# Moving the value bias's product and the key weights' split from the start of the attention stage into the last feed-forward tile

## The chip, the cores and the metric

The kernel runs on one core of one Trainium2 chip. The metric is the time on the device in microseconds (us), as the median of several runs. TensorE is the matrix engine, VectorE, ScalarE and GpSimd are the three engines for elementwise work, and SyncE's queue issues the DMA transfers. In the profile they are PE (with PEld for its weight loads), DVE, ACT, POOL and SP.

## The reference

The input x has 8192 tokens of 512 features. It is normalised, and an attention part and a feed-forward part are added to it:

```
xn  = (x - mean) / sqrt(var + 1e-5)
qkv = xn @ Wqkv + bqkv          # 16 heads of 32
att = softmax(mask(q @ k.T) / sqrt(512)) @ v      # blocks of 128 tokens, each sees itself and its neighbours
h   = bitlinear(xn, w_fc) + gate * (xn @ v.T @ fast_b.T @ u.T)
out = x + (att @ Wout + bout) + bitlinear(relu(h)**2, w_proj)
```

The bias of the values passes through the softmax unchanged, because each row of the softmax sums to one. So the kernel adds it once, as `v_bias @ Wout + bout`, to every token.

## The kernel before

The work runs in three parts, one after the other. A preparation rounds and transposes the feed-forward weights. The feed-forward stage then goes over 16 tiles of 512 tokens and writes x plus its result to the array `partial` in HBM. The attention stage goes over 128 steps (32 pairs of blocks times 4 groups of 4 heads) and adds its own result. A stage is a block in which each engine has an instruction list of its own. No engine starts the next stage before all engines have ended the last one, and SyncE's list in the feed-forward stage ends with waits for all of its stores (L597 to L599).

Every float32 product is made of rounded parts. An operand is split into a high part, rounded by a ScalarE copy, and a low part, which VectorE or GpSimd gets by subtraction. Three products of such parts are then added (hi times hi, lo times hi, hi times lo).

**The feed-forward tile.** It has 16 steps. In step s TensorE makes nine matmuls for `up` (L749 to L753) and, two steps behind, eight for `down` (L763, L765). ScalarE makes `relu` (L643) and the high part of the square (L636). VectorE makes the square (L704) and its low part (L687). At the end of a tile `take_down` (L695, VectorE) scales the four 128-row blocks of `down_ps` into `y`. GpSimd adds the residual x to each block (L611), and SyncE stores each block (L583, for the last tile L596). The first tile and the last tile stand outside the loop, so they can hold instructions of their own. The attention weights `wqkv_raw`, `wout_raw` and the biases are loaded during the first tile.

**The start of the attention stage.** SyncE loads the transposed tokens (L986): first the high part and the low part of block 0, then four more pairs. VectorE spreads the value bias into `v_bias_wide` (L1287). TensorE multiplies it with `wout_raw` in strips of 32 columns (L1523), and VectorE adds `bout_wide` (L1295). Meanwhile ScalarE rounds the keys', the values' and the queries' third of `wqkv_raw`, 128x2048 elements each (L1169), and then `wout_raw` (L1171). VectorE makes the three low parts (L1292), and GpSimd that of `wout` (L1078). After its bias product TensorE makes the keys of block 0 (L1533, 48 matmuls), the values of block 0 (L1362, 12), two jobs of queries and keys (L1353, 48 in all) and the values of block 1 (L1362, 12). Then come the first scores (L1440).

```
            pe.wait_ge(w_lo_done, 1)
            pe.wait_ge(x_here[(-1) % XR], 32)
```

These two waits stand ahead of L1533. The first is for the keys' split and the second for the tokens of block 0.

Of the kernel before, what the change touches and what calls it, by code (L numbers as in the profile page):

```python
# [14 lines left out]
F32 = mybir.dt.float32  # L15
# [7 lines left out]
P = 128  # L23
D = 512
# [426 lines left out]
def feed_forward_stage(nc, x, fast_b, w_fc, w_proj, u, v, gate, xT_dram, x_turned_dram, partial, weights):  # L451
# [13 lines left out]
    with ExitStack() as ctx:  # L465
# [44 lines left out]
        down_ps = ctx.enter_context(nc.psum_tensor("down_ps", [P, NB, D], F32))  # L510
        low_ps = ctx.enter_context(nc.psum_tensor("low_act_ps", [3 * DH, T], F32))

# [7 lines left out]
        xT_stored = [sem(f"xT_stored{b}") for b in range(NB)]  # L520
        block = ctx.enter_context(nc.Block())

        NORM_STEP = [2, 2, 3, 3]
# [21 lines left out]
        def _(sp):  # L545
# [55 lines left out]
        @block.gpsimd  # L601
        def _(pool):
            def tile(i, par):

                if not is_last(i):
                    for b in range(NB):
                        inverse_std(pool, nc, stats[:, b, :], minus_half, ln_step[b], 5 * (i + 1) + 3)
                for b in range(NB):
                    pool.wait_ge(down_taken, NB * i + b + 1)
                    pool.wait_ge(part_here[b], 16 * (i + 1))  # L610
                    nc.gpsimd.tensor_tensor(y[:, b, :], y[:, b, :], part_in[:, b, :], ALU.add).then_inc(y_done, 1)  # L611

            tiles(pool, tile)

        @block.scalar
        def _(act):
# [11 lines left out]
            def low_high(i, par):  # L628
                act.wait_ge(low_filled, i + 1)
                nc.scalar.copy(low[:, par, :], low_ps[:, :]).then_inc(low_hi_done, 1)  # L630

# [6 lines left out]
            def tile(i, par):  # L638
                for s in range(FB):
# [21 lines left out]
        def _(dve):  # L661
# [36 lines left out]
            def tile(i, par):  # L698
                for s in range(FB):
# [26 lines left out]
            square_lo(NT - 1, FB - 1)  # L726
            take_down(NT - 1)

        @block.tensor
        def _(pe):  # L730
            def low_rank(i, par):
# [3 lines left out]
                for n in range(2 * DC):  # L735
                    k, pass_ = divmod(n, 2)
                    a = xT_lo if pass_ else xT_hi
                    last = nc.tensor.matmul(low_ps[:, :], low_in[:, k, :], a[:, par, k, :],
                                            start=(n == 0), stop=(n == 2 * DC - 1))
# [40 lines left out]
            for s in range(FB - LAG, FB):  # L780
                down(NT - 1, s)


def attention_stage(nc, loaded, xT_dram, partial, turned_dram, pair_dram, out):
# [14 lines left out]
    with ctx:  # L799
# [7 lines left out]
        wqkv_here, wout_here, biases_here = loaded.arrived  # L807
        wqkv_hi = sb("wqkv_hi", [P, DC, 3 * D], F32R)
        wqkv_lo = sb("wqkv_lo", [P, DC, 3 * D], F32R)
        wout_hi = sb("wout_hi", [P, DC, D], F32R)  # L810
        wout_lo = sb("wout_lo", [P, DC, D], F32R)
        v_bias_wide = sb("v_bias_wide", [P, DC, P], F32)
        out_bias = sb("out_bias", [P, D], F32)
        mask = sb("mask", [P, 3 * P], F32)
# [29 lines left out]
        wout_hi_done, wout_lo_done = sem("wout_hi_done"), sem("wout_lo_done")  # L844
        wide_done, bias_summed, bias_added = sem("v_bias_wide_done"), sem("bias_summed"), sem("bias_added")
        zeroed, ident_done, mask_done = sem("ident_zeroed"), sem("ident_done"), sem("mask_done")
# [23 lines left out]

        SPLIT_ORDER = (1, 2, 0)

# [195 lines left out]
        def _(pool):  # L1068
# [6 lines left out]
                                    fill=NEG, base=0, pattern=[[-1, P]], channel_multiplier=1).then_inc(mask_done, 1)  # L1075
            pool.wait_ge(bias_summed, 1)
# [3 lines left out]
            pool.wait_ge(bias_added, 1)  # L1080

            def widen_inverse_sums(t, b):
# [38 lines left out]
        def _(act):  # L1121
# [44 lines left out]
            act.wait_ge(wqkv_here, 64)  # L1166
            for part in SPLIT_ORDER:
                cols = slice(part * D, (part + 1) * D)
                nc.scalar.copy(wqkv_hi[:, :, cols], wqkv_raw[:, :, cols]).then_inc(w_hi_done, 1)  # L1169
            act.wait_ge(wout_here, 16)  # L1170
# [29 lines left out]
        def _(dve):  # L1200
# [85 lines left out]
            dve.wait_ge(biases_here, 48)  # L1286
            nc.vector.tensor_copy(v_bias_wide[:, :, :], v_bias[:, :].unsqueeze(2).to_broadcast([P, DC, P])  # L1287
                                  ).then_inc(wide_done, 1)
            for n, part in enumerate(SPLIT_ORDER):
                cols = slice(part * D, (part + 1) * D)  # L1290
                dve.wait_ge(w_hi_done, n + 1)
                nc.vector.tensor_tensor(wqkv_lo[:, :, cols], wqkv_raw[:, :, cols],  # L1292
                                        wqkv_hi[:, :, cols].bitcast(F32), ALU.subtract).then_inc(w_lo_done, 1)
            dve.wait_ge(bias_summed, 1)
            nc.vector.tensor_tensor(out_bias[:, :], score_ps[:, 0, :], bout_wide[:, :], ALU.add).then_inc(bias_added, 1)  # L1295
            dve.wait_ge(mask_done, 2)
# [38 lines left out]
        def _(pe):  # L1335
# [7 lines left out]
            def project_qk(u, bank, first, last_):  # L1343

                i, c = where(u)
                for n in range(first, last_):
                    is_k, m = divmod(n, PASSES * DC)
                    k, x_low, w_low = pass_of(m)
                    w = wqkv_lo if w_low else wqkv_hi
                    a = xT_lo if x_low else xT_hi  # L1350
                    col = is_k * D + c * P
                    tokens = a[:, x_slot(i):x_slot(i) + 2, k, :] if is_k else own_tokens(a, i, k)
# [4 lines left out]
            def project_v(i, r, bank, first, last_):  # L1357
                for n in range(first, last_):
                    k, x_low, w_low = pass_of(n)
                    w = wqkv_lo if w_low else wqkv_hi  # L1360
                    a = xT_lo if x_low else xT_hi
                    last = nc.tensor.matmul(job_ps[:, bank, :], a[:, x_slot(i) + r, k, :], w[:, k, 2 * D:3 * D],  # L1362
                                            start=(n == 0), stop=(n == PASSES * DC - 1))
# [153 lines left out]

            pe.wait_ge(wide_done, 1)
            pe.wait_ge(wout_here, 16)
            for k in range(DC):  # L1520
                for g in range(HC):
                    strip = slice(g * DH, (g + 1) * DH)
                    last = nc.tensor.matmul(score_ps[strip, 0, :], v_bias_wide[:, k, strip], wout_raw[:, k, :],  # L1523
                                            start=(k == 0), stop=(k == DC - 1), tile_position=(0, g * DH))
            last.then_inc(bias_summed, 1)
            pe.wait_ge(w_lo_done, 1)
            pe.wait_ge(x_here[(-1) % XR], 32)
            for c in range(DC):
                for n in range(PASSES * DC):
                    k, x_low, w_low = pass_of(n)  # L1530
                    w = wqkv_lo if w_low else wqkv_hi
                    a = xT_lo if x_low else xT_hi
                    last = nc.tensor.matmul(job_ps[:, 0, c * P:(c + 1) * P], w[:, k, D + c * P:D + (c + 1) * P],  # L1533
                                            a[:, x_slot(-1) + 1, k, :], start=(n == 0), stop=(n == PASSES * DC - 1))
# [42 lines left out]
class AttentionWeights:  # L1577
# [3 lines left out]
    sources: tuple  # L1581
    tables: tuple
    arrived: tuple

# [22 lines left out]
def feed_forward(nc, x, partial, fast_b, w_fc, w_proj, u, v, gate, out):  # L1607
# [6 lines left out]
    with ExitStack() as ctx:  # L1614
# [3 lines left out]
        def sem(name):  # L1618
# [3 lines left out]
                                   (sb("wqkv_raw", [P, DC, 3 * D]), sb("wout_raw", [P, DC, D]),  # L1622
                                    sb("v_bias", [P, DC]), sb("qk_bias", [P, 2 * DC]), sb("bout_wide", [P, D])),
                                   (sem("wqkv_here"), sem("wout_here"), sem("biases_here")))
        feed_forward_stage(nc, x, fast_b, w_fc, w_proj, u, v, gate, xT_dram, x_turned_dram, partial, weights)
# [34 lines left out]
```

## Time and profile before

| | |
|---|---|
| median of 3 runs | 2405.69 us (2405.29 to 2405.75) |
| the profiled execution's own time | 2402.34 us |
| its span, first to last instruction | 2400.5 us |
| mean granted TensorE clock | 0.992 of full speed |
| TensorE busy | 2341.3 us (98%) |
| VectorE, ScalarE, GpSimd busy | 1675.9, 1374.2, 441.6 us |
| preparation and feed-forward stage | from 0 to 1095.2 us |
| attention stage | from 1095.2 us to the end |

Times in the rows are counted from the start of the span. The granted clock is a share of full speed: 1.00 is 2.4 GHz and 0.50 is 1.2 GHz. Instructions on one engine overlap a little at their ends, so the busy time of a group can be less than its count times its mean.

### The profile page before, as it was taken

How to read it: one execution, taken by the hardware profiler on the slowest of the kernel's cores; microseconds unless marked ns; L12 is line 12 of the kernel's file. 1: busy time of each engine (PE TensorE's matmuls, PEld its weight loads, DVE VectorE, ACT ScalarE, POOL GpSimd, SP SyncE). 2: the span in 40 equal slices, each digit the busy share in tenths (PEclk: the TensorE clock that was granted, in tenths of full speed). 3: DMA queues.
4: the chain of work that ended last, by engine and by line, in shares of the span. 5: the costliest groups of instructions: out<-in, count | busy, mean ns of one | idle time of the engine just before them, and what ended most of it. 6: DMA issues, size and time to landing. Idle time of an engine off the chain costs nothing.

```text
span 2400.5 us, 56237 instructions
## 1 busy us (share of the span) xinstructions
PE 2341.3 (98%) x19528; PEld 1912.8 (80%) x19528; DVE 1675.9 (70%) x4576; ACT 1374.2 (57%) x3488; POOL 441.6 (18%) x734
## 2 busy tenths in 40 slices
PE   6999999999999999998999999999999999999997
PEld 5888888888888888886788888888887888888885
DVE  6455544555545444535888888888888888988896
ACT  6333333333333333324777777777777777777775
POOL 2011111111111001102222222222222222222222
PEclk8999999999999999999999999999999999999999
DMA  5643344433344444314899999999999999999996
GB/s 188 206 113 110 102 114 122 117 102 109 110 122 122 114 113 122 105 36 133 261 293 296 292 296 291 290 300 283 298 289 294 293 292 288 294 291 290 291 286 191
DMA packets 390109, 495.74 MB, mean 207 GB/s; under 512 B 35792, under 2 KB 296400, under 8 KB 389888
## 3 DMA queue, kind: packets, MB, share of 16 engines
q1 hardware_dynamic: 389744, 492.71, 69.7%
q8 instruction: 129, 2.11, 0.4%
q14 instruction: 92, 0.75, 0.1%
q0 software_dynamic: 144, 0.17, 0.0%
HBM read 261.53 MB, written 231.21 MB: 205 GB/s over the span
## 4 chain that ended last, share of the span: by engine, by line
PE 27%; DMA 9%; ACT 7%; issue 4%; DVE 4%; SPq 2%; POOL 0%; POOLq 0%; DVEq 0%
PE job_ps L1353 8%; PE job_ps L1362 5%; PE job_ps L1513 5%; ACT wqkv_raw L1134 5%; PE score_ps L1440 4%; DMA turned_pairs<-pair_blocks 4%; DMA pair_moved<-turned_pairs 3%; PE job_ps L1371 3%; DVE wqkv_raw L1212 2%; PE pT_ps L1456 2%; SPq L1035 1%; DMA turned_blocks<-wqkv_raw 1%; ACT pT L1143 1%; DMA wqkv_raw<-turned_blocks 1%; ACT q_hi L1159 1%
## 5 line engine op out<-in xcount | busy, mean ns | idle before, releaser
L1134 ACT ACTIVATE wqkv_raw<-wqkv_raw,neg_max 128x384 f32<-128x384 f32 (+1 forms) x1024 | 619.3, 606 | 218.8 <-DVE neg_max L1212 215.8
L643 ACT ACTIVATE relu<-up_ps,fc_scale 128x512 f32<-128x512 f32 x256 | 176.1, 688 | 633.5 <-PE up_ps L753 633.5
L704 DVE SCALAR_TENSOR_TENSOR sq<-up_ps,relu 128x512 f32<-128x512 f32 x256 | 177.0, 692 | 494.5 <-ACT relu L643 493.3
L1212 DVE CUSTOM_DVE_ANT_0 wqkv_raw<-score_ps,mask 128x384 f32<-128x384 f32 (+1 forms) x1024 | 504.0, 549 | 25.1 <-PE score_ps L1440 24.2
L765 PE MATMUL down_ps<-proj_T,sq_lo 128*128 128x512 f32 x1024 | 404.7, 395 | 0.0
L763 PE MATMUL down_ps<-proj_T,sq_hi 128*128 128x512 f32 x1024 | 404.3, 395 | 0.2 <-DVE sq_lo L687 0.2
L749 PE MATMUL up_ps<-f_xT_hi,fc_T 128*128 128x512 f32 x1024 | 400.3, 391 | 2.2 <-PEq L136 2.2
L751 PE MATMUL up_ps<-f_xT_lo,fc_T 128*128 128x512 f32 x1024 | 400.3, 391 | 0.0
L1229 DVE STREAM_TRANSPOSE wqkv_raw<-wqkv_raw 128x384 f32<-128x384 f32 (+1 forms) x508 | 282.6, 573 | 66.9 <-ACT wqkv_raw L1134 64.2
L1353 PE MATMUL job_ps<-xT_hi,wqkv_hi 128*128 128x256 f32 x1024 | 309.9, 303 | 0.1
L1353 PE MATMUL job_ps<-xT_lo,wqkv_hi 128*128 128x256 f32 x1024 | 289.2, 282 | 0.0
L1353 PE MATMUL job_ps<-xT_hi,wqkv_lo 128*128 128x256 f32 x1024 | 288.9, 282 | 0.0
L611 POOL TENSOR_TENSOR f_y<-f_y,part_in 128x512 f32<-128x512 f32 x64 | 88.2, 1410 | 865.5 <-DVE f_y L695 865.5
L763 PEld LDWEIGHTS down_ps<-proj_T,sq_hi 128*128 128x128 f32 x1024 | 193.7, 189 | 45.6 <-DVE sq_lo L687 1.1
L765 PEld LDWEIGHTS down_ps<-proj_T,sq_lo 128*128 128x128 f32 x1024 | 192.8, 188 | 45.6
L749 PEld LDWEIGHTS up_ps<-f_xT_hi,fc_T 128*128 128x128 f32 x1024 | 192.7, 188 | 44.7 <-issue 2.4
L751 PEld LDWEIGHTS up_ps<-f_xT_lo,fc_T 128*128 128x128 f32 x1024 | 192.9, 188 | 43.5
L1087 POOL COPY rcp_wide<-sum_rcp 128x128 f32<-128x128 f32 x256 | 74.7, 292 | 805.7 <-DVE sum_rcp L1221 805.7
L1353 PEld LDWEIGHTS job_ps<-xT_lo,wqkv_hi 128*128 128x128 f32 x1024 | 196.3, 192 | 0.0
L1353 PEld LDWEIGHTS job_ps<-xT_hi,wqkv_hi 128*128 128x128 f32 x1024 | 195.5, 191 | 0.5 <-ACT values L1127 0.3
L1353 PEld LDWEIGHTS job_ps<-xT_hi,wqkv_lo 128*128 128x128 f32 x1024 | 195.3, 191 | 0.0
L1134 ACT ACTIVATION_READ_ACCUMULATOR wqkv_raw<-wqkv_raw,neg_max 128x1 f32 x1024 | 192.5, 188 | 0.0
(158 smaller groups left out, 4374.3 us busy)
## 6 DMA issues: line engine op xcount, KB each, us to landing
turned_blocks<-wqkv_raw SPq DMA_DIRECT2D x123, 768.0 KB, 4.8
wqkv_raw<-turned_blocks SPq DMA_DIRECT2D x492, 192.0 KB, 4.1
turned_pairs<-pair_blocks SPq DMA_DIRECT2D x124, 384.0 KB, 4.1
pair_moved<-turned_pairs SPq DMA_DIRECT2D x496, 96.0 KB, 3.3
xT_hi<-xT SPq DMA_DIRECT2D x65, 256.0 KB, 4.9
xT_lo<-xT SPq DMA_DIRECT2D x65, 256.0 KB, 5.0
xT<-f_xT_hi SPq DMA_DIRECT2D x64, 256.0 KB, 2.9
xT<-f_xT_lo SPq DMA_DIRECT2D x64, 256.0 KB, 3.1
```

The source lines that it names most:

```text
L643: nc.scalar.activation(relu[:, s % 2, :], up_ps[:, s % 2, :], ACT.Relu, scale=fc_scale2[:, s:s + 1]).then_inc(relu_done, 1)
L704: nc.vector.scalar_tensor_tensor(sq[:, s % 2, :], up_ps[:, s % 2, :], 0.0, relu[:, s % 2, :], ALU.max, ALU.mult).then_inc(sq_done, 1)
L749: nc.tensor.matmul(up_ps[:, s % 2, :], fc_T[:, k, cols], xT_hi[:, par, k, :], start=(k == 0), stop=False)
L751: nc.tensor.matmul(up_ps[:, s % 2, :], fc_T[:, k, cols], xT_lo[:, par, k, :], start=False, stop=False)
L763: nc.tensor.matmul(down_ps[:, b, :], sq_hi[:, s % 2, t], proj_T[:, s, :], start=(s == 0), stop=False)
L765: last = nc.tensor.matmul(down_ps[:, b, :], sq_lo[:, s % 2, t], proj_T[:, s, :], start=False, stop=(s == FB - 1))
L1134: nc.scalar.activation(probs[:, u, cols], probs[:, u, cols], ACT.Exp, bias=neg_max[:, u:u + 1], scale=-1.0, accum_out=prob_sum[:, u:u + 1] ...
L1212: nc.vector.tensor_tensor_reduce(out=probs[:, u, cols], in0=score_ps[:, h, cols], in1=mask[:, cols], scale=-SCORE_SCALE, scalar=3e38, op0= ...
L1229: nc.vector.transpose(blocks[:, :, seen.start:seen.stop, u, :].rearrange("p a w t -> p w a t"), probs[:, u, seen.start * P:seen.stop * P]. ...
L1353: last = nc.tensor.matmul(job_ps[:, bank, is_k * T:(is_k + 1) * T], w[:, k, col:col + P], tokens, start=(m == 0), stop=(m == PASSES * DC - 1))
L1362: last = nc.tensor.matmul(job_ps[:, bank, :], a[:, x_slot(i) + r, k, :], w[:, k, 2 * D:3 * D], start=(n == 0), stop=(n == PASSES * DC - 1))
L1513: last = nc.tensor.matmul(out_, values[:, blk % VR, head * DH:(head + 1) * DH], p, start=(w == seen.start), stop=(w == seen.stop - 1), til ...
```

## The change

- **Bias product.** `v_bias_wide` is made by VectorE in step 4 of the last feed-forward tile. TensorE makes the product after the last `down` step of that tile, as four matmuls over all 128 columns instead of sixteen over 32, into `low_ps`. VectorE adds `bout_wide` at the end of its list. In the attention stage L1287, L1523 and L1295 go.
- **Key weights.** ScalarE rounds the keys' third of the weights in four pieces of 128x512, in steps 4 to 7 of the last tile. VectorE makes the low part in four pieces in steps 5 to 8. The attention stage splits only values and queries.
- **Residual blocks.** Of the last tile's four blocks GpSimd adds 0 and 1. VectorE adds 2 and 3 after `take_down`. SyncE stores them in the order 0, 2, 1, 3.
- **Waits.** In the attention stage TensorE's waits for `wide_done` and `wout_here`, the first one for `w_lo_done`, and that for `bias_added` go, as do GpSimd's for `bias_summed` and `bias_added`.

```diff
@@ SyncE, feed-forward stage
-            for b in range(NB):
-                sp.wait_ge(y_done, NB * (NT - 1) + b + 1)
+            for b in (0, 2, 1, 3):
+                if b < 2:
+                    sp.wait_ge(y_done, NB * (NT - 1) + b + 1)
+                else:
+                    sp.wait_ge(late_y_done, b - 1)
                 sp.dma_start(block_rows(partial, NB * (NT - 1) + b), y[:, b, :]).then_inc(stored[b], 16)
@@ GpSimd
-                for b in range(NB):
+                for b in range(2 if is_last(i) else NB):
@@ ScalarE, step s
+                    if is_last(i) and 0 <= s - W_STEP < DC:
+                        act.wait_ge(wqkv_here, 64)
+                        nc.scalar.copy(wk_hi[:, s - W_STEP, :], wqkv_raw[:, s - W_STEP, KEY_COLS]).then_inc(w_rounded, 1)
@@ VectorE, step s
+                    if is_last(i) and s == W_STEP:
+                        dve.wait_ge(biases_here, 48)
+                        nc.vector.tensor_copy(v_bias_wide[:, :, :], v_bias[:, :].unsqueeze(2).to_broadcast([P, DC, P])
+                                              ).then_inc(wide_done, 1)
+                    if is_last(i) and 0 <= s - W_STEP - 1 < DC:
+                        k = s - W_STEP - 1
+                        dve.wait_ge(w_rounded, k + 1)
+                        nc.vector.tensor_tensor(wk_lo[:, k, :], wqkv_raw[:, k, KEY_COLS], wk_hi[:, k, :].bitcast(F32),
+                                                ALU.subtract)
@@ VectorE, after the last take_down
+            for b in range(2, NB):
+                dve.wait_ge(down_taken, NB * (NT - 1) + b + 1)
+                dve.wait_ge(part_here[b], 16 * NT)
+                nc.vector.tensor_tensor(y[:, b, :], y[:, b, :], part_in[:, b, :], ALU.add).then_inc(late_y_done, 1)
+            dve.wait_ge(bias_summed, 1)
+            nc.vector.tensor_tensor(bout_wide[:, :], low_ps[:, :], bout_wide[:, :], ALU.add)
@@ TensorE, after the last down
+            pe.wait_ge(wide_done, 1)
+            pe.wait_ge(wout_here, 16)
+            for k in range(DC):
+                last = nc.tensor.matmul(low_ps[:, :], v_bias_wide[:, k, :], wout_raw[:, k, :], start=(k == 0), stop=(k == DC - 1))
+            last.then_inc(bias_summed, 1)
@@ attention stage, TensorE
-            pe.wait_ge(wide_done, 1)
-            pe.wait_ge(wout_here, 16)
-            for k in range(DC):
-                for g in range(HC):
-                    strip = slice(g * DH, (g + 1) * DH)
-                    last = nc.tensor.matmul(score_ps[strip, 0, :], v_bias_wide[:, k, strip], wout_raw[:, k, :],
-                                            start=(k == 0), stop=(k == DC - 1), tile_position=(0, g * DH))
-            last.then_inc(bias_summed, 1)
-            pe.wait_ge(w_lo_done, 1)
             pe.wait_ge(x_here[(-1) % XR], 32)
...
-            pe.wait_ge(w_lo_done, 2)
+            pe.wait_ge(w_lo_done, 1)
...
-            pe.wait_ge(w_lo_done, 3)
+            pe.wait_ge(w_lo_done, 2)
...
-            pe.wait_ge(bias_added, 1)
@@ attention stage, ScalarE and VectorE: two splits instead of three
-        SPLIT_ORDER = (1, 2, 0)
+        SPLIT_ORDER = ((slice(2 * D, 3 * D), slice(D, 2 * D)), (slice(0, D), slice(0, D)))
```

The split weights stand in other tensors than before: `wk_hi`, `wk_lo` (128x4x512) are held from the feed-forward stage on, and `wqv_hi`, `wqv_lo` (128x4x1024) belong to the attention stage. `v_bias_wide` moves to the feed-forward stage, and the attention stage's `out_bias` is now `bout_wide`.

## Rows read from the trace of the kernel before

**Rows 1.** Windows: us, then busy us (instructions) of each engine, granted clock, DMA share, GB/s.

```profile
1086.90:1090.20 3.30, 0.00 (x0) 0.00 (x0) 2.48 (x4) 0.00 (x0) 2.51 (x3) 1.00 0.11 43
1090.40:1095.70 5.30, 0.00 (x0) 0.00 (x0) 0.45 (x1) 0.48 (x1) 2.55 (x4) 0.50 0.42 157
1095.70:1100.60 4.90, 4.86 (x24) 1.18 (x28) 3.45 (x2) 4.90 (x3) 1.06 (x4) 0.50 0.89 281
...
1101.70:1118.50 16.80, 16.80 (x124) 15.49 (x120) 5.63 (x10) 4.22 (x10) 7.11 (x5) 1.00 0.25 85
...
1200.00:1400.00 200.00, 199.14 (x2345) 164.37 (x2347) 178.43 (x561) 148.41 (x435) 46.59 (x90) 1.00 0.99 294
```

**Rows 2.** Timeline between the stages: start us, us, engine, line, operation [idle before].

```profile
1086.92 2.48 DVE L695 TENSOR_TENSOR f_y<-down_ps,proj_scale 128x512 f32<-128x512 f32 x4 [2.77 <-PE down_ps L765]
1087.69 4.92 POOL L611 TENSOR_TENSOR f_y<-f_y,part_in 128x512 f32<-128x512 f32 x4 [53.44 <-DVE f_y L695]
1088.98 3.99 SPq L596 DMA_DIRECT2D partial<-f_y  x4
...
1095.20 0.34 SPq L986 DMA_DIRECT2D xT_hi<-xT  x1
...
1095.59 0.43 SPq L986 DMA_DIRECT2D xT_lo<-xT  x1
```

**Rows 3.** Source lines of stores and loads: us from issue to landing.

```profile
L596 SPq DMA_DIRECT2D partial<-f_y x4: 332/338/343, 1089.0 to 1092.6; - x4
...
DMA to landing us min/median/max: 2.0/2.0/2.0
...
L986 SPq DMA_DIRECT2D xT_lo<-xT x1: 427/427/427, 1095.6 to 1095.6; - x1
...
DMA to landing us min/median/max: 3.0/3.2/3.4
```

**Rows 4.** Chain of waits at the attention stage's start: start us, us, what.

```profile
1095.24 0.46 DVE v_bias_wide L1287
...
1095.74 6.03 PE score_ps L1523 x32
1101.77 5.51 PE job_ps L1533 x48
```

**Rows 5.** Timeline of ScalarE and VectorE in a step of the last tile.

```profile
1076.96 0.69 ACT L643 ACTIVATE relu<-up_ps,fc_scale 128x512 f32<-128x512 f32 x1 [2.73 <-PE up_ps L753]
1077.55 0.61 ACT L636 CAST sq_hi<-sq 128x512 fp32r<-128x512 f32 x1
...
1077.68 0.69 DVE L704 SCALAR_TENSOR_TENSOR sq<-up_ps,relu 128x512 f32<-128x512 f32 x1 [2.64 <-ACT relu L643]
```

**Rows 6.** VectorE and GpSimd together, tiles 1 and 15: timeline, source L611.

```profile
126.40 1.78 DVE L687 TENSOR_TENSOR sq_lo<-sq,sq_hi 128x512 fp32r<-128x512 f32 x1
...
L611 POOL TENSOR_TENSOR f_y<-f_y,part_in x1: 1292/1292/1292, 126.3 to 126.3; 128x512 f32<-128x512 f32 x1
...
1031.17 0.68 DVE L687 TENSOR_TENSOR sq_lo<-sq,sq_hi 128x512 fp32r<-128x512 f32 x1
...
L611 POOL TENSOR_TENSOR f_y<-f_y,part_in x1: 1805/1805/1805, 1031.2 to 1031.2; 128x512 f32<-128x512 f32 x1
```

**Rows 7.** Source lines of the weight splits: ns minimum/median/maximum, starts.

```profile
L1169 ACT CAST wqkv_hi<-wqkv_raw x3: 1893/1895/1899, 1095.2 to 1098.8; 128x2048 fp32r<-128x2048 f32 x3
...
L1292 DVE TENSOR_TENSOR wqkv_lo<-wqkv_raw,wqkv_hi x3: 2284/2286/2292, 1097.1 to 1101.6; 128x2048 fp32r<-128x2048 f32 x3
```

**Rows 8.** TensorE in the preparation: timeline, then windows.

```profile
23.00 1.06 PE L340 MATMUL first_ps<-f_ident,f_x_in 128*128 128x128 f32 x4
23.85 1.06 PE L376 MATMUL turn_ps<-f_ident,fc_in 128*128 128x128 f32 x4
...
32.00:32.40 0.40, 0.40 (x5) 0.40 (x4) 0.40 (x1) 0.00 (x0) 0.00 (x0) 0.70 0.00 0
```

More of the change, by code:

```diff
@@ L510, in feed_forward_stage @@
         down_ps = ctx.enter_context(nc.psum_tensor("down_ps", [P, NB, D], F32))
-        low_ps = ctx.enter_context(nc.psum_tensor("low_act_ps", [3 * DH, T], F32))
+        low_ps = ctx.enter_context(nc.psum_tensor("low_act_ps", [P, T], F32))
+        v_bias_wide = sb("v_bias_wide", [P, DC, P])
+        wqkv_raw, wout_raw, v_bias, _, bout_wide = weights.tables
+        wk_hi, wk_lo = weights.parts
+        wqkv_here, wout_here, biases_here = weights.arrived
+        w_rounded, wide_done, bias_summed = sem("w_rounded"), sem("v_bias_wide_done"), sem("bias_summed")
+        late_y_done = sem("late_y_done")
         part_here = [sem(f"part_here{b}") for b in range(NB)]
@@ L521, in feed_forward_stage @@
         block = ctx.enter_context(nc.Block())
+        W_STEP = 4
+        KEY_COLS = slice(D, 2 * D)
         NORM_STEP = [2, 2, 3, 3]
@@ L629, in low_high @@
                 act.wait_ge(low_filled, i + 1)
-                nc.scalar.copy(low[:, par, :], low_ps[:, :]).then_inc(low_hi_done, 1)
+                nc.scalar.copy(low[:, par, :], low_ps[0:3 * DH, :]).then_inc(low_hi_done, 1)
             def square_hi(i, s):
@@ L737, in low_rank @@
                     a = xT_lo if pass_ else xT_hi
-                    last = nc.tensor.matmul(low_ps[:, :], low_in[:, k, :], a[:, par, k, :],
+                    last = nc.tensor.matmul(low_ps[0:3 * DH, :], low_in[:, k, :], a[:, par, k, :],
                                             start=(n == 0), stop=(n == 2 * DC - 1))
@@ L807, in attention_stage @@
         wqkv_here, wout_here, biases_here = loaded.arrived
-        wqkv_hi = sb("wqkv_hi", [P, DC, 3 * D], F32R)
-        wqkv_lo = sb("wqkv_lo", [P, DC, 3 * D], F32R)
+        wk_hi, wk_lo = loaded.parts
+        wqv_hi = sb("wqv_hi", [P, DC, 2 * D], F32R)
+        wqv_lo = sb("wqv_lo", [P, DC, 2 * D], F32R)
         wout_hi = sb("wout_hi", [P, DC, D], F32R)
         wout_lo = sb("wout_lo", [P, DC, D], F32R)
-        v_bias_wide = sb("v_bias_wide", [P, DC, P], F32)
-        out_bias = sb("out_bias", [P, D], F32)
+        out_bias = bout_wide
         mask = sb("mask", [P, 3 * P], F32)
@@ L1079, in _ @@
                                     ALU.subtract).then_inc(wout_lo_done, 1)
-            pool.wait_ge(bias_added, 1)
             def widen_inverse_sums(t, b):
@@ L1166, in _ @@
             act.wait_ge(wqkv_here, 64)
-            for part in SPLIT_ORDER:
-                cols = slice(part * D, (part + 1) * D)
-                nc.scalar.copy(wqkv_hi[:, :, cols], wqkv_raw[:, :, cols]).then_inc(w_hi_done, 1)
+            for part, own in SPLIT_ORDER:
+                nc.scalar.copy(wqv_hi[:, :, own], wqkv_raw[:, :, part]).then_inc(w_hi_done, 1)
             act.wait_ge(wout_here, 16)
@@ L1286, in _ @@
             dve.wait_ge(biases_here, 48)
[L1287 to L1290, printed above, removed]
+            for n, (part, own) in enumerate(SPLIT_ORDER):
                 dve.wait_ge(w_hi_done, n + 1)
[L1292 to L1295, printed above, removed]
+                nc.vector.tensor_tensor(wqv_lo[:, :, own], wqkv_raw[:, :, part], wqv_hi[:, :, own].bitcast(F32),
+                                        ALU.subtract).then_inc(w_lo_done, 1)
             dve.wait_ge(mask_done, 2)
@@ L1359, in project_v @@
                     k, x_low, w_low = pass_of(n)
-                    w = wqkv_lo if w_low else wqkv_hi
+                    w = wqv_lo if w_low else wqv_hi
                     a = xT_lo if x_low else xT_hi
-                    last = nc.tensor.matmul(job_ps[:, bank, :], a[:, x_slot(i) + r, k, :], w[:, k, 2 * D:3 * D],
+                    last = nc.tensor.matmul(job_ps[:, bank, :], a[:, x_slot(i) + r, k, :], w[:, k, D:2 * D],
                                             start=(n == 0), stop=(n == PASSES * DC - 1))
@@ L1530, in _ @@
                     k, x_low, w_low = pass_of(n)
-                    w = wqkv_lo if w_low else wqkv_hi
+                    w = wk_lo if w_low else wk_hi
                     a = xT_lo if x_low else xT_hi
-                    last = nc.tensor.matmul(job_ps[:, 0, c * P:(c + 1) * P], w[:, k, D + c * P:D + (c + 1) * P],
+                    last = nc.tensor.matmul(job_ps[:, 0, c * P:(c + 1) * P], w[:, k, c * P:(c + 1) * P],
                                             a[:, x_slot(-1) + 1, k, :], start=(n == 0), stop=(n == PASSES * DC - 1))
             last.then_inc(job_filled, 1)
-            pe.wait_ge(w_lo_done, 2)
+            pe.wait_ge(w_lo_done, 1)
             project_v(-1, 1, 1, 0, PASSES * DC).then_inc(job_filled, 1)
             pe.wait_ge(k0_done, 1)
-            pe.wait_ge(w_lo_done, 3)
+            pe.wait_ge(w_lo_done, 2)
             pe.wait_ge(x_here[0], 64)
@@ L1582 @@
     tables: tuple
+    parts: tuple
     arrived: tuple
```

7 lines of the change are left out of this document (3 added, 4 removed).

## The prediction

> **What bounds the kernel now.** I read the windows first, because they tell which stages have room. In the attention stage TensorE is busy 199 of 200 us at full clock and the DMA engines 0.99 of the time [rows 1]. The change leaves that loop alone, and in the feed-forward tiles it only fills waits of other engines (step 1). It touches the seam between the two stages, and there the reader sees two gaps. From 1086.9 us, the end of the last `down` matmul, to 1095.7 TensorE does nothing, and its granted clock falls from 1.00 to 0.50 inside that gap. It stays at 0.50 (1.2 GHz) until 1100.6, and from 1101.7 to 1118.5 TensorE works without a break at 1.00 [rows 1]. The timeline then says who holds the first gap: `take_down` ends at 1089.4, GpSimd's four adds end at 1092.6, the last store is issued at 1088.98 + 3.99 - 0.33 = 1092.64, and the next stage starts at 1095.20 [rows 2]. The store lands 2.0 us after its issue [rows 3], at 1094.65, so the seam itself costs 0.55. The chain of waits tells what comes next: 0.46 for `v_bias_wide`, 6.03 for the bias product, then the keys of block 0 from 1101.77 [rows 4]. Everything behind follows TensorE without a gap up to the first scores, so time won or lost ahead of L1533 is won or lost at the end, one to one.
>
> **Step 1, the work put into the last tile.** In each step of about 3.9 us (2.73 + 0.69 + 0.61, less a small overlap) ScalarE waits 2.73 us for `up` and VectorE 2.64 us for ScalarE [rows 5]. ScalarE gets four copies of 128x512, each like its 0.61 us copy of the square [rows 5]. VectorE gets four subtractions of 0.68 [rows 6] and one spread of 0.46 [rows 4]. One of these per step fits into the wait with 2 us to spare, and TensorE needs their results only at the end of the tile. Cost 0, by the cover of the `up` matmuls. Without that cover it would be at most 4 x 0.68 + 0.46 = 3.2 us.
>
> **Step 2, the bias product behind the last `down`.** The old product is 32 instructions in 6.03 us [rows 4]. The strips run side by side: four 32-column pieces make one 128-column group, so these are 8 groups. At half clock a group starts every 0.85 us and at full clock every 0.43, as 8 groups in 6.03 us with 4.9 at half clock require (4.9 / 0.85 = 5.8 groups, and 2.2 x 0.43 = 0.95). The new form is the same 8 groups over all columns. TensorE comes straight from `down` at full clock, so it ends at 1086.8 + 8 x 0.43 = 1090.3. If the full clock were not granted, it would end at 1093.6. VectorE's add behind it takes 0.68 like the other reads of PSUM. Both stay ahead of the stores (step 3), so this costs 0. At half clock it would just reach them.
>
> **Step 3, the residual blocks.** `take_down` is unchanged, and VectorE is ready for block 2 at about 1089.3. If the two adds ran freely, at 0.62 from start to start, all blocks would be done at 1090.65 and the seam would come about 1.9 us earlier. But GpSimd is then inside its add of block 1, from 1088.9 to 1090.15, and both operations read two tensors of SBUF. In tile 1 a VectorE subtraction of this kind started at 126.40, while a GpSimd add had run since 126.3. It took 1.78 us instead of 0.68, and the GpSimd add took its usual 1.29. In the last tile the order was the other way round: the subtraction, started at 1031.17, took 0.68, and the GpSimd add behind it took 1.81 [rows 6]. So the later one waits until the earlier one is done. `take_down` reads PSUM and SBUF, and it ran beside GpSimd with no loss (4.92 / 4 = 1.23 for each add) [rows 2]. I therefore let block 2 wait for block 1: block 1 at 1090.15, block 2 at 1090.75, block 3 at 1091.35.
>
> The stores are issued in the order 0, 2, 1, 3, so three of them follow each other at 1090.8, 1091.2 and 1091.55 instead of one every 1.23 us. Alone a store lands after 2.0 us. In the loads of the next stage the second of two transfers issued 0.39 apart took 3.4 us where the first took 3.0 [rows 3]. The fourth store therefore lands between 1093.55 (no crowding) and 1094.35 (0.4 for each of two ahead). I take 1094.0, against 1094.65: **0.65 us won**, with bounds 0.3 and 1.1, and 1.9 without any hold.
>
> The Trainium skill (GPSIMD Engine Reference, Specifications) says that GpSimd's SBUF interfaces are shared with VectorE, with contention when a VectorE instruction has two SBUF inputs. The trace agrees (1.78 us for 0.68). A reader without this rule would book 1.9 us for this step, and I book 0.65.
>
> **Step 4, the start of the attention stage.** L1533 waited for the bias product, until 6.57 us after the stage's start [rows 4]. Now only the tokens hold it. Their second transfer is issued 0.39 after the start and lands after 3.4 us [rows 2, 3], so TensorE starts at 3.8: **2.75 us won**. The next wait, for the values' split, is not late. ScalarE's copy ends at 1.9 and VectorE's subtraction of 2.29 at 4.2 [rows 7], while TensorE needs it at 9 or later. The queries' split follows at 6.5 and is needed at 12. GpSimd starts the low part of `wout` 1.9 us earlier, since ScalarE has one copy less. SyncE's queue is in the same order as before, and the DMAs behind it keep their distance to the stage's start.
>
> **Step 5, what the bias product also did.** It ran while the clock was at 0.50, and so the keys' matmuls found the clock full. After the change TensorE stops at 1090.3 and starts again at 1094.55 + 3.8 = 1098.3, after 8 us. In the gap of before, the clock was down by 1090.4, 3.5 us after the last matmul [rows 1], so I expect 0.50 at the restart. A 128x128 matmul then starts every (23.85 - 23.00) / 4 = 0.2125 us [rows 8], against 5.41 / 48 = 0.113 at full clock [rows 4]. Each us at half clock thus loses 0.47 us. The full clock came 4.9 us after the restart before the old bias product [rows 1]. In the preparation, after a restart at 29.03, it came at 32.2 (the window 32.0 to 32.4 shows 0.70) [rows 8]. The two lengths are 3.2 and 4.9 us, and I take 4.2: **2.0 us lost** (1.5 to 2.3).
>
> The Trainium skill (TensorE: Matmul & The Clock Gate, "What's actually happening") says that the number of matmuls that run cold varies from run to run. The trace shows two such lengths, 3.2 and 4.9, and with the one the sum would be 0.5 us better than with my 4.2, with the other 0.3 us worse.
>
> **Sum.** 0.65 + 2.75 - 2.0 = 1.4 us won. The profiled execution would fall from 2402.34 to 2400.9 us. It stands 3.35 us under the median of the runs, and the difference applies to the median alike: 2405.69 - 1.4 = **2404.3 us**, 0.06% less. What a measurement of this kernel can tell from no change is 0.2%, or 4.8 us.
>
> **The rivals.**
> - *The clock does not fall, or comes back at once.* The matmuls of the bias product shorten the idle time by 3.5 us. Then nothing is lost in step 5, and the gain is 3.4, time 2402.3. Against it: the gap still lasts 8 us, and the clock was down within 3.5. Chance 0.08.
> - *The splits and blocks bring what they could at most.* No hold between VectorE and GpSimd, and a full clock: 1.9 + 2.75 = 4.65, time 2401.0. Still under 0.2%. Against it: the waits of [rows 6]. Chance 0.03.
> - *Slower: the clock stays down.* The 48 matmuls of block 0 keep TensorE less densely at work than the bias product, whose instructions stream 512 columns. If the clock stays at 0.50 through the whole 16.8 us of work up to the first scores, that work takes 33.6 at most, and the sum is 3.4 - 16.8 = 13.4 us slower, time 2419. It decides from 3.4 / 0.47 = 7.2 us of half clock on. Against it: transposes of the same shape brought the clock back in 3.2 us. Chance 0.04 for beyond 7.2 us, most of it small.
> - *The split does nothing.* If the tokens landed as late as the bias product ended, step 4 would be 0. The loads were issued at 1095.2 and 1095.6 and landed by 1099.0, so this has 0.02. The time would be 2407.0 (0.65 won, 2.0 lost).
> - *The loops themselves move.* Tensors of the attention stage lie elsewhere, and with TensorE and the DMA engines both full, 0.3% in either direction would be 4 us of the 1300 us stage. No row shows such a thing. Chance 0.12, half to each side, and half of that beyond 0.2%.
>
> **How the numbers follow.** My forecast has 0.71. Its own range takes the bounds together: the gain is at least 0.3 + 2.5 - 2.6 = 0.2 and at most 1.9 + 2.9 - 1.5 = 3.3, so 2402.4 to 2405.5. To leave out no more than 2 in 10 the range goes to 2401.5 and 2406.5. Faster by over 0.2% needs more than 4.8 us, more than all steps at their best, so it has only the loops' share and a little more: 0.06. Slower by over 0.2% has the clock and the loops: 0.05. The rest, 0.89, is no difference.
>
> **What would show it.** Right: a granted clock of 0.50 under the first keys' matmuls, which then start every 0.21 us, and L1533 at 3.8 us after the stage's start. Also a VectorE add of block 2 of about 1.4 us while GpSimd's add keeps 1.27, and a stage start 0.65 us earlier, at about 1094.55. Also ScalarE's and VectorE's new instructions inside waits of the last tile, with TensorE unbroken there. Wrong: two adds of 0.68 back to back, a clock of 1.00 at L1533, or steps of the attention loop of another length than before.

## The result and the profile after

The changed kernel is slower: 2409.95 us median (2402.26 to 2418.84, 22 runs) against 2404.4 for the kernel before on the same chips (2399.15 to 2413.66, 22 runs). The ratio is 1.0026, 95% interval 1.0017 to 1.0035. The forecast was 2404.3, with 2401.5 to 2406.5, and it stood on the three runs' median of 2405.69: 1.4 us faster, where the medians here say 5.5 us slower. The profiled execution has a span of 2406.6 us, against 2400.5.

The windows of the changed kernel, from the start of the attention stage to the first scores (the columns are those of [rows 1]):

```profile
1097.50:1101.70 4.20, 0.00 (x0) 0.00 (x0) 1.87 (x1) 3.87 (x3) 1.40 (x5) 0.52 0.73 220
1101.70:1112.00 10.30, 10.25 (x48) 10.25 (x49) 2.62 (x2) 1.63 (x1) 5.30 (x1) 0.50 0.63 218
1112.00:1114.30 2.30, 2.30 (x8) 1.82 (x8) 0.69 (x3) 1.14 (x4) 0.00 (x0) 0.50 0.00 0
1114.30:1115.00 0.70, 0.70 (x4) 0.56 (x3) 0.44 (x2) 0.00 (x0) 0.00 (x0) 0.68 0.00 0
1115.00:1124.70 9.70, 9.70 (x66) 8.74 (x64) 1.75 (x4) 2.27 (x5) 1.49 (x4) 1.00 0.00 0
```

TensorE works without a gap from 1101.7 on, and still the granted clock stays at 0.50 (1.2 GHz) until 1114.75 (a mean of 0.68 over the window from 1114.3 means 0.45 us of it at 0.50). That is 13.0 us, under all 48 matmuls of block 0's keys and 2.7 us into the wider ones of its values. (The expectations below say 12.7, read from coarser windows.) In [rows 1] that clock came back inside the bias product. The chain of waits shows the price (start us, us, what):

```profile
1097.91 3.79 DMA xT_lo<-xT
...
1101.75 10.50 PE job_ps L1549 x48
1112.25 4.03 PE job_ps L1387 x12
1116.28 5.75 PE job_ps L1378 x48
```

L1549 is the L1533 of before, and L1387 its L1362. The keys took 5.51 us [rows 4] and now take 10.50. The values took 2.83 in the chain of the kernel before and now take 4.03. That makes 6.2 us lost. The timeline of the seam has the steps of [rows 2]:

```profile
1089.50 3.59 PE L815 MATMUL low_act_ps<-wout_raw,v_bias_wide 128*128 128x512 f32 x8
1089.70 2.48 DVE L710 TENSOR_TENSOR f_y<-down_ps,proj_scale 128x512 f32<-128x512 f32 x4 [2.77 <-PE down_ps L795]
...
1090.47 2.49 POOL L623 TENSOR_TENSOR f_y<-f_y,part_in 128x512 f32<-128x512 f32 x2 [53.44 <-DVE f_y L710]
...
1091.76 3.08 SPq L608 DMA_DIRECT2D partial<-f_y  x4
...
1092.10 2.01 DVE L755 TENSOR_TENSOR f_y<-f_y,part_in 128x512 f32<-128x512 f32 x2
1094.03 0.68 DVE L757 TENSOR_TENSOR bout_wide<-low_act_ps,bout_wide 128x512 f32<-128x512 f32 x1
1097.52 0.20 POOL L69 MEMSET ident<- 128x128 f32 x1 [4.56 <-POOLq L465]
```

From the end of the last `down` (0.39 us behind its start, at 1089.66) to the next stage are now 7.86 us, against 8.32: 0.46 won. From there to the keys are 4.23 us, against 6.57: 2.3 won. So the seam as a whole lost 6.2 - 0.46 - 2.3 = 3.4 us. The other 2.8 us by which this profile is longer up to the first scores lie ahead of the seam: the last `down` ends at 1089.66 instead of 1086.88. Whether the change makes that difference is one question of the experiments.

### The profile page after: what moved, and what is told of

Its sections match the earlier page's. It is cut to its first block, busy times and chain, and to the rows that moved or that the text cites. A ratio compares the mean times of both kernels' runs of the same rounds, so it can differ in the third digit from the quotient of the medians.

```text
span 2406.6 us, 56193 instructions
## 1 busy us (share of the span) xinstructions
PE 2344.6 (97%) x19504; PEld 1921.4 (80%) x19504; DVE 1677.2 (70%) x4581; ACT 1374.6 (57%) x3491; POOL 438.7 (18%) x732
## 4 chain that ended last, share of the span: by engine, by line
PE 34%; DMA 7%; ACT 5%; issue 3%; DVE 3%; SPq 1%; POOL 0%; POOLq 0%; DVEq 0%
PE job_ps L1378 10%; PE job_ps L1387 6%; PE job_ps L1538 6%; PE score_ps L1465 5%; PE job_ps L1396 4%; ACT wqkv_raw L1165 3%; DMA turned_pairs<-pair_blocks 3%; DMA pair_moved<-turned_pairs 3%; PE pT_ps L1481 3%; DVE wqkv_raw L1242 2%; SPq L1069 1%; ACT pT L1174 1%; PE pT_ps L1485 1%; ACT q_hi L1190 0%; ACT k_hi L1193 0%
## 5 line engine op out<-in xcount | busy, mean ns | idle before, releaser
L702 DVE TENSOR_TENSOR sq_lo<-sq,sq_hi 128x512 fp32r<-128x512 f32 x256 | 175.7, 686 | 0.6 <-ACT sq_hi L648 0.6
L648 ACT CAST sq_hi<-sq 128x512 fp32r<-128x512 f32 x256 | 156.7, 612 | 0.8 <-PE down_ps L795 0.7
L1378 PE MATMUL job_ps<-xT_hi,wqv_hi 128*128 128x256 f32 x512 | 155.5, 304 | 0.1
L1378 PE MATMUL job_ps<-xT_hi,wk_hi 128*128 128x256 f32 x512 | 155.0, 303 | 0.0
L1174 ACT COPY pT<-pT_ps 128x512 f32<-128x512 f32 x256 | 144.9, 567 | 3.0 <-PE pT_ps L1485 3.0
L1378 PE MATMUL job_ps<-xT_lo,wqv_hi 128*128 128x256 f32 x512 | 145.1, 283 | 0.0
```

The costliest lines, as they stand in the source:

```text
L702: nc.vector.tensor_tensor(sq_lo[:, s % 2, :], sq[:, s % 2, :], sq_hi[:, s % 2, :].bitcast(F32), ALU.subtract).then_inc(sq_lo_done, 1)
L1174: nc.scalar.copy(pT[:, h - MOVED, seen.start:4, :].rearrange("p w t -> p (w t)"), pT_ps[:, h % 2, seen.start * P:4 * P]).then_inc(pT_done, 1)
L1378: last = nc.tensor.matmul(job_ps[:, bank, is_k * T:(is_k + 1) * T], w[:, k, col:col + P], tokens, start=(m == 0), stop=(m == PASSES * DC - 1))
```

## The experiments

In all of them the first and the second half of the kernel are read apart. "First scores" is the distance from the attention stage's start to its first score matmul: 23.3 us in the kernel before, 27.2 in the changed one.

**Keeping TensorE at work through the seam.** To the changed kernel:

```diff
             last.then_inc(bias_summed, 1)
+            for _ in range(15):
+                nc.tensor.matmul(up_ps[:, 0, :], fc_T[:, 0, 0:P], xT_hi[:, 1, 0, :], start=True, stop=True)
...
+            for _ in range(16):
+                nc.tensor.matmul(score_ps[:, 0, :], wk_hi[:, 0, 0:P], wk_hi[:, 0, :], start=True, stop=True)
             pe.wait_ge(x_here[(-1) % XR], 32)
```

> The changed kernel with matmuls added whose results nobody reads: 15 of 512 columns behind the bias product and 16 ahead of the wait for block 0's tokens, so that TensorE hardly rests between the stages. Clock theory (the keys of block 0 ran at 1.2 GHz because TensorE had rested and narrow matmuls do not bring the clock back): the granted clock stays at 1.00 through the seam, the 48 keys' matmuls take 5.4 us instead of 10.5 and the values 2.8 instead of 4.0, so about 6 us less than the changed kernel and 2.5 to 3 us less than the kernel before. Placement theory (tensors that lie elsewhere make the preparation 2.6 us later): the preparation stays as late as in the changed kernel, 2.8 us behind the kernel before, and the whole is level with the kernel before.

Measured: 2406.78 us, ratio to before 1.0007 (0.9996 to 1.0018). By the medians more than half of the loss is gone, and not all. Windows of this kernel:

```profile
1091.00:1101.00 10.00, 8.00 (x33) 5.75 (x31) 4.88 (x5) 4.63 (x3) 1.91 (x6) 1.00 0.58 202
1101.10:1103.00 1.90, 1.89 (x17) 1.89 (x17) 1.77 (x1) 0.77 (x1) 1.04 (x1) 1.00 0.93 299
1103.10:1109.60 6.50, 6.50 (x33) 6.50 (x32) 0.00 (x0) 0.00 (x0) 4.16 (x1) 0.50 0.60 212
1109.70:1113.80 4.10, 4.10 (x12) 3.24 (x12) 1.12 (x4) 1.14 (x4) 0.00 (x0) 0.56 0.09 34
```

The clock was full through the seam and under the first 17 keys' matmuls. It then fell in the middle of them, with no gap in TensorE's work since 1101.1 and one of 1.1 us ahead of it, and came back only 3.7 us into the values' wide matmuls (at 1113.3). The expectation of 5.4 us for the keys is wrong. They took 8.5, and the first scores came at 26.7. That is only 0.5 us sooner than in the changed kernel, so the seam of this profile does not carry the difference between the medians, and the rest of it is unexplained.

**The bias product back in its place,** with the keys' split and the residual blocks as in the change:

```diff
-            for k in range(DC):
-                last = nc.tensor.matmul(low_ps[:, :], v_bias_wide[:, k, :], wout_raw[:, k, :], ...)
+            # attention stage, ahead of the wait for x_here: spread, product and add as in the kernel before
```

> The changed kernel with the bias product back at the start of the attention stage; the keys' split and the two residual blocks stay where the change put them. Clock theory: the product again absorbs the half clock (6.0 us), the keys take 5.4 us, the seam keeps its 0.45 us, so 0.5 us faster than the kernel before, no more. Placement theory: the weights lie in other tensors as in the changed kernel, so the preparation ends about 2.6 us late and the kernel is 2 us slower than before.

Measured: 2403.38 us, ratio 0.9992 (0.9984 to 1.0001). The chain of waits has the keys at full speed again:

```profile
1098.15 4.96 PE score_ps L1545 x32
1103.11 5.50 PE job_ps L1554 x48
```

The keys take 5.3 us from first to last start, and the first scores come at 22.2, 1.1 sooner than before. The product took 4.96 us here instead of 6.03, since the clock came back sooner (2.7 us after the product's start instead of 4.9), and that makes the 1.1. The loss belongs to the product's move. The rest of the change costs nothing, and the interval does not show a gain either.

**The values of block 0 ahead of its keys,** in the changed kernel (ScalarE reads the two results in the new order too):

```diff
+            pe.wait_ge(w_lo_done, 1)
+            project_v(-1, 1, 1, 0, PASSES * DC).then_inc(job_filled, 1)
             for c in range(DC):
...
-            pe.wait_ge(w_lo_done, 1)
-            project_v(-1, 1, 1, 0, PASSES * DC).then_inc(job_filled, 1)
```

> The changed kernel with the values of block 0 (12 matmuls of 512 columns) ahead of its keys (48 of 128 columns); nothing else. If narrow matmuls keep the clock down, the full clock comes some 3 to 5 us after the restart, during or just behind the wide values, and the half clock lasts under 6 us instead of 12.7: about 4 us less than the changed kernel. If the length of the half clock is only a matter of time since the restart, it lasts 12 us again and the time is that of the changed kernel.

Measured: 2410.42 us, ratio 1.0022 (1.0012 to 1.0031), no better than the change. The clock half of the expectation held and the time did not. The chain of waits, and in the second block the windows:

```profile
1101.52 5.30 PE job_ps L1387 x12
1106.82 5.32 PE job_ps L1551 x48
1112.17 1.15 ACT k_hi L1206 x4
1113.37 0.07 issue
1113.43 1.14 DVE k_lo L1324 x4
1114.61 8.44 PE job_ps L1378 x48
```

```profile
1101.50:1106.20 4.70, 4.68 (x11) 3.73 (x12) 2.07 (x1) 1.08 (x1) 3.54 (x1) 0.50 0.92 328
...
1112.20:1114.90 2.70, 0.29 (x1) 0.29 (x2) 1.12 (x4) 1.11 (x4) 0.00 (x0) 0.71 0.00 0
1114.90:1120.00 5.10, 5.10 (x25) 5.10 (x25) 0.00 (x0) 0.00 (x0) 0.00 (x0) 0.50 0.00 0
```

Behind 5.0 us of 512-column matmuls the clock came back, and the 48 keys ran at full clock. But the next job needs the keys' split, which the values used to cover. TensorE waited 2.5 us for it. The clock fell again at 1113.3, after 5.3 us of keys and 1.2 us of that wait, and the jobs of 256 columns took 8.44 us instead of 5.75.

**The residual blocks alone,** in the kernel before:

```diff
-                for b in range(NB):
+                for b in range(2 if is_last(i) else NB):
                     pool.wait_ge(down_taken, NB * i + b + 1)
...
+            for b in range(2, NB):
...
+                nc.vector.tensor_tensor(y[:, b, :], y[:, b, :], part_in[:, b, :], ALU.add).then_inc(late_y_done, 1)
```

> The kernel before with one part of the change alone: VectorE adds residual blocks 2 and 3 of the last tile, stores in the order 0, 2, 1, 3. VectorE's first add waits for GpSimd's (about 1.4 us instead of 0.68), the next stage starts 0.4 to 0.7 us earlier behind the last down matmul, and nothing else moves: 0.5 us faster. A rival that books two free adds expects 1.9 us. Placement theory: tensors lie as before, so the preparation ends as in the kernel before, at 52.2 us.

Measured: 2404.97 us, ratio 0.9998 (0.9989 to 1.0007), which cannot tell 0.5 us from nothing. In the profile the stage starts 8.2 us behind the start of the last `down` matmul instead of 8.7. The two free adds' 1.9 us are not there.

**A seam with wide work throughout.** The split and the blocks as in the change, the bias product at the head of the attention stage as four full-width matmuls, 30 unread matmuls behind the last `down` and one behind the product:

```diff
+            for _ in range(30):
+                nc.tensor.matmul(up_ps[:, 0, :], fc_T[:, 0, 0:P], xT_hi[:, 1, 0, :], start=True, stop=True)
...
+                last = nc.tensor.matmul(score_ps[:, 0, :], v_bias_wide[:, k, :], wout_raw[:, k, :],
+                                        start=(k == 0), stop=(k == DC - 1))
```

> The split and the residual blocks as in the change, but the bias product at the head of the attention stage, as four matmuls over all columns, with 30 matmuls of 512 columns whose results nobody reads behind the last down matmul and one behind the product. Density theory (128-column matmuls do not hold the clock up or bring it back; wide ones do, and the bias product was the wide work in front of the keys): clock 1.00 from the last down matmul through the product (3.5 us) and the keys (5.4 us), keys from 4.3 us after the stage's start, first scores at 21.1 us behind it against 23.3 before, so 2.6 us faster than the kernel before. If the clock falls inside the keys in spite of that, as it did with the first filler, the keys take 8 us and the kernel is level with before.

Measured: 2402.59 us, ratio 0.9995 (0.9984 to 1.0005). The granted clock is 1.00 in every microsecond from the last `down` to the first scores, and those come at 22.1. TensorE rested 1.6 us ahead of the product and 0.7 us behind its filler, and neither pause brought the clock down. The tokens landed late in this profile (4.8 us behind their issue), which took 0.9 of the expected 2.2.

**Wide and narrow dealt.** In the changed kernel three wide matmuls of the values behind every twelve of the keys:

```diff
+                last_v = project_v(-1, 1, 1, 3 * c, 3 * c + 3)
```

> The changed kernel with the 12 wide matmuls of block 0's values dealt among its 48 narrow keys' matmuls, three behind every twelve; no work added. Density theory: the clock is up again only when enough wide work has run, somewhat sooner than in the changed kernel (12.7 us at half clock), perhaps 7 to 12 us. A theory in which any dense stream brings the clock back after 3 to 5 us expects no difference to the changed kernel, since that stream was without a gap as well.

Measured: 2413.92 us, ratio 1.0038 (1.0023 to 1.0053), worse than the change. The clock stays at 0.50 until 1124.1, for 22.6 us from the first key, and the first scores come at 32.0. Both theories expected less. The order also uncovers the wait for the keys' split, here 1.2 us, and that pause lies inside the 22.6:

```profile
1101.50:1117.10 15.60, 15.60 (x60) 14.00 (x60) 2.88 (x2) 3.02 (x6) 5.32 (x1) 0.50 0.46 159
1117.20:1118.30 1.10, 0.00 (x0) 0.00 (x0) 1.10 (x4) 0.59 (x1) 0.00 (x0) 0.50 0.00 0
1118.40:1124.10 5.70, 5.70 (x27) 5.70 (x28) 0.00 (x0) 0.22 (x1) 0.00 (x0) 0.50 0.00 0
```

So the mix alone left the clock at 0.50 for 15.6 us. What it would have done without the pause is not shown.

**The keys twice.** The 48 keys' matmuls of the changed kernel are made a second time, and the output is the same:

```diff
+            for c in range(DC):
+                for n in range(PASSES * DC):
+                    ...     # the same matmuls again
```

> The changed kernel with the 48 narrow keys' matmuls of block 0 made twice; the output is the same. Density theory: the clock stays at 0.50 through all 96 of them, some 20 us, and comes back 2 to 5 us into the wide matmuls behind; the first scores come 10 us later than in the changed kernel. Theory of a fixed time (12.7 us after the restart): the clock comes back at about 12.7 us, amid the second 48, and the first scores come only some 6 us later.

Measured in one run: 2422.73 us. Windows:

```profile
1101.40:1121.60 20.20, 20.20 (x96) 20.20 (x96) 2.81 (x2) 1.82 (x2) 5.31 (x1) 0.50 0.35 119
1121.60:1126.50 4.90, 4.90 (x13) 3.90 (x13) 1.13 (x4) 1.14 (x4) 0.00 (x0) 0.50 0.00 0
1126.60:1130.00 3.40, 3.40 (x28) 3.34 (x27) 0.00 (x0) 0.59 (x1) 0.00 (x0) 0.96 0.00 0
```

TensorE is busy 20.20 of 20.20 us with 96 narrow matmuls, and the clock does not move from 0.50. It rises at 1126.9, 5.1 us into the 512-column matmuls and 25.7 us after the restart, and the first scores come 10.9 us later than in the changed kernel. A fixed time after the restart is ruled out.

**The change once more,** with no edit:

> The changed kernel once more, for a second profile. If the half clock under the keys is systematic, the keys take 9 to 10.5 us again. If the later preparation (54.8 against 52.2 us for the first up matmul) is chance, this profile has another value. From the seam alone the kernel is 0.45 + 2.3 us better and 6.2 us worse, 3.4 us slower than before.

Measured: 2408.49 us, ratio 1.0019 (1.0008 to 1.0030). The keys take 10.1 us from first to last start and the first scores come at 27.1. The first `up` matmul starts at 53.8 us instead of 54.8.

**Tensors moved, nothing else,** in the kernel before:

```diff
+        with nc.sbuf_tensor("pad", [P, 2 * DC, D], F32):
             feed_forward_stage(nc, x, fast_b, ...
```

> The kernel before with 16 KB per partition that nobody uses held in SBUF ahead of the feed-forward part's tensors, as the change's two weight tensors are; nothing else. Placement theory: in the eight profiles with those tensors the first up matmul starts at 53.6 to 54.8 us, in the two without at 52.2 and 52.7, so it starts here near 54.3 and the kernel is some 1.8 us (0.08%) slower. If that difference is chance, or comes from elsewhere in the change, it starts near 52.5 and the time is that of the kernel before.

Measured: 2399.99 us against 2399.94 on this chip, ratio 0.9998 (0.9989 to 1.0007), first `up` at 52.2. The shifted tensors cost nothing that the interval can tell. The three other kernels measured with it are not shifted and have their first `up` at 53.5 to 54.8, so the preparation varies by up to 2.6 us between profiles without the shift. Of the 2.8 us ahead of the seam, 2.6 lie in the preparation and within that spread. With one profile of each kernel a smaller systematic part is not excluded.

**Filler and product in place,** in the kernel before: the 30 unread matmuls and the full-width product as above, and the residual blocks on VectorE.

> The kernel before with three edits: the two residual blocks on VectorE, the bias product in its old place but as four matmuls over all columns, and 30 matmuls of 512 columns, whose results nobody reads, behind the last down matmul. The keys' split stays where it was. Clock at 1.00 throughout, product 3.7 us, keys from about 4.5 us behind the stage's start (held by the keys' split, 4.2, and the tokens), first scores 22 us behind it against 23.3, seam 0.45 shorter: 1.8 us faster than the kernel before, and with the first up matmul at 52.5 us also faster than the version that keeps the change's split.

Measured: 2398.79 us, ratio 0.9993 (0.9984 to 1.0002). In the profile the first scores come at 21.1, 2.2 us sooner than before, and the seam is 0.45 shorter. The clock is 1.00 throughout. Chain of waits:

```profile
1096.87 1.91 ACT wqkv_hi L1179
1098.77 0.02 issue
1098.80 2.30 DVE wqkv_lo L1302
1101.10 0.04 issue
1101.14 5.58 PE job_ps L1541 x48
```

The keys' split, left in the attention stage, is ready 4.25 us after the stage's start. In the changed kernel the tokens were there after 4.2. So moving the split gained almost nothing. The product's move alone, next, has the keys at 4.36 with the split in its old place.

**The product's move alone,** in the kernel before:

```diff
+            for k in range(DC):
+                last = nc.tensor.matmul(low_ps[:, :], v_bias_wide[:, k, :], wout_raw[:, k, :], start=(k == 0), stop=(k == DC - 1))
...
-                    last = nc.tensor.matmul(score_ps[strip, 0, :], v_bias_wide[:, k, strip], wout_raw[:, k, :],
-                                            start=(k == 0), stop=(k == DC - 1), tile_position=(0, g * DH))
```

> The kernel before with one part of the change alone: the bias product behind the last down matmul of the feed-forward part (with its spread in step 4 and its add at the end). Density theory: the keys, which still start when their split and tokens are there (4.3 us after the stage's start), run at 1.20 GHz throughout, 10.1 us, and the first scores come 27.2 us behind the stage's start against 23.3: 3.9 us slower than before. If another part of the change made the loss, this one is 2.2 us faster.

(The "1.20 GHz" there is the lower of the two clock levels, 1.2 GHz.) Measured: 2406.52 us against 2399.94, ratio 1.0025 (1.0016 to 1.0034). Within the noise this single part makes the whole loss (ratio 1.0026 and 1.0019 for the full change). The chain of waits has the 10.5 us again:

```profile
1100.03 2.30 DVE wqkv_lo L1302
1102.34 0.04 issue
1102.38 10.50 PE job_ps L1533 x48
1112.88 3.69 PE job_ps L1370 x12
```

**The kernel before once more,** with no edit:

> The kernel before once more, for a second profile of it. The clock theory expects the bias product to take 5 to 6 us again, with the full clock back inside it, and the keys 5.3 us. The placement theory expects the first up matmul near 52.5 us; a value of 54 or later would put that difference down to chance.

Measured in one run: 2399.8 us. The product takes 5.86 us, the keys 5.51 in the chain of waits, and the first scores come at 23.2. The first `up` starts at 53.5, between the two values that the expectation named, so this profile decides nothing about placement. The shifted kernel's 52.2, and 54.2 and 54.8 in the two others without the shift, speak against it.

## Why the prediction was wrong, step by step

- **Step 1, the work put into the last tile: right.** Between the first `up` and the last `down` lie 1034.4 us, against 1034.3 before. Twelve other profiles have 1034.2 to 1034.9.
- **Step 2, the product behind the last `down`: right in itself.** It took 3.59 us (3.5 expected) and did not hold the stores.
- **Step 3, the residual blocks: right in its mechanism, 0.46 us won for 0.65.** The two VectorE adds took 2.01 us together, the first of them 1.41, while GpSimd's block took 1.27. The later one waited for the earlier, as in [rows 6]. From the end of the last `down` the last store was issued 1.0 us earlier than before, where 1.1 was forecast, and the slowest of the four took 2.6 us to land instead of 2.0. Booked as free, the step would have been overstated by 1.4 us.
- **Step 4, the earlier start of the keys: 2.3 us won for 2.75.** The second token transfer landed after 3.8 us instead of 3.4. Nearly all of it came from the product's move (keys at 4.36 with that alone) and hardly any from the split's.
- **Step 5, "2.0 us lost (1.5 to 2.3)": this term failed.** The half clock was expected at the restart, and at the right rate: 0.2125 us for a 128x128 matmul, measured 0.213. Its length was wrong, 13.0 us instead of 4.2, and so the price is 6.2 us. The range did not cover this, though its sum took 2.6 as the largest loss where the step's own bound is 2.3. I had taken the length from the bias product (512 columns) and from transposes in the preparation. The work that now stood at the restart was of another kind: float32r matmuls of 128 columns. Under those the clock did not come back in any profile, not in 10 us and not in 20. The slower rival described this with 7.2 us as its deciding point. It got 0.04, and the objection raised against it (the transposes) was the error.

The transposes looked like a fair stand-in because they have the keys' shape and, at half clock, the keys' spacing of 0.213 us. But in the version with the values first, at half clock, the float32r matmuls of 256 columns also started every 0.213 us (its window from 1114.9), and those of 512 columns every 0.427 (from 1101.5). The keys have half the columns of the former and are no faster, so their columns do not set their spacing, and an equal spacing was no sign of equal work. Nor do 128 columns by themselves explain it, since the transposes have 128 too and the clock came back under them. Which property of the keys it is stays open: no run varied the type or the weight loads at a fixed number of columns.

The Trainium skill (TensorE: Matmul & The Clock Gate, "What's actually happening") calls the warm-up a matter of time and not of a number of matmuls. The doubled keys disagree: the same unbroken stream for 20.2 us left the clock at 0.50.

With 6.2 in place of 2.0, and the measured 0.46 and 2.3, the steps give 3.4 us slower. The medians say 5.5 and 4.0 in the two measurements of the change, and 6.6 for the product's move alone, where the profile accounts for 3.8 against the second profile of the kernel before. The 95% intervals reach down to 4.1, 1.9 and 3.8 us. So 0.6 to 2.8 us may be missing, and their cause is open. From the first to the last score matmul the three profiles behind these numbers have 1257.2, 1258.3 and 1258.2 us, and the two of the kernel before 1257.4 and 1253.6. No experiment took that apart.

The other runs have no rows, but each has its span and its mean granted clock. The share below full speed, times the span, averages 23.0 us over the 11 runs of the change's second measurement, against 18.0 over 23 runs of the kernel before. For the product's move alone it is 24.1, against 18.8. The seams of the profiles account for 3.4 of these 5.0 and 5.3: 17.1 us at half clock instead of 10.2, counted half. So some runs may spend more time at half clock than the profiled ones. The means are uncertain by about 1 us each, so this is a hint and not shown.

## What to carry to other kernels

Work that TensorE does while it waits anyway can be what brings its clock back, so before moving it, ask which matmuls then stand at the restart, and take the length of the half clock from rows with that same kind of matmul. A gain of a few microseconds at one seam is smaller than the spread of single runs here (2399 to 2414 us for one kernel), so it has to be read in the profiles, stage by stage. The best version tried kept the product where it was and filled the gap with wide matmuls. Its profile shows 2.7 us won at the seam (2.5 against the second profile of the kernel before), and its interval (0.9984 to 1.0002) does not exclude zero.

## What the runs showed of the hardware

- 48 and 96 float32r matmuls of 128 columns, back to back at 1.2 GHz, left the granted clock at 0.50 for 10.3 and 20.2 us. It rose 2.0 to 5.1 us into the 512-column matmuls behind them, in four profiles.
- The clock also fell under such matmuls, 2 us into an unbroken stream of them and 3.1 us behind the last wide matmul. In eight other profiles, where wide matmuls stood 0.7 us or less ahead of them, it stayed at 1.00 under the same 48 for 5.3 us. What decides between the two was not found.
- Twelve wide matmuls dealt among the 48 narrow ones did not bring it back either. It stayed at 0.50 through 15.6 us of the mix, a pause of 1.2 us and 5.7 us of 256-column matmuls.
